# A vision tower on one core: value heads as stationaries of 32 or 64 columns, dealt over the strips of the array

## The chip, the cores and the metric

The kernel is written in Bass and runs on one core of a Trainium2 chip. A core has TensorE (PE, with its weight loads listed as PEld), VectorE (DVE), ScalarE (ACT), GpSimd (POOL), and SyncE (SP), which issues the transfers. The metric is the device time of one execution in microseconds (us).

## The reference

64 images of 84 by 84 pixels become 26 tokens each (a class token and 25 patches) of 192 features. Four layers follow, each an attention and a feed-forward block with a residual sum, all in fp32. Layer 2 has an attention inside its feed-forward block and so has layer 3, which makes six attentions. With `q`, `k`, `v` the projections of the normalised tokens, the part that matters here is the same in all six:

```
attn = einsum('bhqd,bhkd->bhqk', q, k)              # the scores, per image and head
attn = softmax / causal softmax / relative softmax / random features / integer softmax of it
out  = einsum('bhqk,bhkd->bhqd', attn, v)           # the value products
out  = out.transpose(0, 2, 1, 3).reshape(b, n, -1) @ proj_w + proj_b
```

| attention | heads x width | kind | time of it in the profile, us |
|---|---|---|---|
| L0 | 6 x 32 | causal, low rank | 76 to 163 |
| L1 | 12 x 64 | softmax with tables of relative positions for scores and values | 1662 to 1950 |
| L2a | 12 x 16 | random features (no exponent of the scores) | 2152 to 2304 |
| L2f | 12 x 16 | softmax | 2330 to 2427 |
| L3a | 12 x 16 | integer softmax, on VectorE alone | 2755 to 2857 |
| L3f | 12 x 16 | softmax, and a mix of tokens by a score, on GpSimd | 2884 to 3020 |

## The kernel before, in words

Everything is planned by hand: each engine has its own list of steps, and semaphores tie them. `attention()` writes all six attentions. It works on tiles of four images (4 x 26 = 104 tokens), 16 tiles in all. Four tiles make a turn (two in L1), so there are four turns (eight in L1). The lists `order` (PE, ACT) and `dve_order` (DVE) fix what comes after what within a turn, for instance on PE: values 0, v 2, scores 3, k, q, values 1, v 3, out of the last turn, scores 0 of the next, values 2, v 0, back, scores 1, values 3, v 1, back, scores 2. Engines are strictly in order, so a step that waits holds up all behind it.

The steps of one tile:

- **scores** (PE, L1673): for each image `im` (0 to 3) and each chunk `c` of heads (`NC` chunks: 2 in L0, L2f, L3a, L3f; 4 in L2a; 6 in L1), one product with a stationary of 32 columns (the image's 26 queries and padding). Its output goes to rows 32 `im` to 32 `im` + 31 of the bank, so `im` picks a strip of 32 columns of the array. The loop runs over images outside and chunks inside. In L1 `rel_scores` (L1683) does the same with a table of 40 columns.
- **shift, normalise** (DVE): subtract the maximum, sum, reciprocal, scale, transpose in blocks of 32. `exponents` (ACT) lies between them in the softmax kinds. In L1 both parts have some twenty small instructions more.
- **blocks** (ACT L1906, POOL L1622): the transposed weights of the four images are copied into a block-diagonal operand `p_bd` (in `n_tok`) of 104 rows and 104 columns per head.
- **v** (PE L595, then ACT L1888 and L1890, or L1895 in L1): the values of the tile are projected and written to `v_x`. Each head has 128 columns there, of which only its own 16 (32, 64) are not zero: the zeros are cleared once (POOL L1342, L1388) and the values are put at the place of the head among the output's rows. The last third of the heads is written twice, because the output projection wants those 64 rows in both halves.
- **values** (PE L1704): for each head one product of its 128 columns of `v_x` with `p_bd`, 104 columns, summed in PSUM over 8 heads, then over 4 heads. In L1 two heads and a product with the table `rel_table` (L1724) make one sum, six times. ACT L1943 or L1946 moves the result to `o_f`.
- **out, back**: the output projection, its transposes, and the sum with the residual on DVE (L2230).
- **spread** (DVE L2077): writes the keys of the next turn, one copy for each head with all other heads' rows zero. Scores of the next turn wait for it (`k_done`).

An fp32 product shows as two matrix passes in the trace, each with its own weight load: a tile of L2f has 12 products, 24 passes.

Of the kernel before, what the change touches and what calls it, by code (L numbers as in the profile page):

```python
# [25 lines left out]
IMG, SLOT = 64, 26  # L26
# [74 lines left out]
def vit_tower(nc, a, out, stop=99):  # L101
# [17 lines left out]
    with ctx:  # L119
# [68 lines left out]
        k_x = sb("k_x", [128, 12 * 416], scope=at)  # L188
        v_x = sb("v_x", [128, 2 * 1536 + 128], scope=at)
        z_t = [sb(f"z_t{j}", [128, 12, SLOT], scope=at) for j in range(2)]  # L190
# [1211 lines left out]
        def attention(cfg, res, *others, stats_too=True):  # L1402
# [132 lines left out]

            def spots(j, at, copies, copy_step, heads, step):
                part = v_x[:, 1536 * j + at:1536 * j + at + 1]
                return bass.AP(part.tensor, part.offset, [part.ap[0], [copy_step, copies], [step, heads], [1, d]])

# [107 lines left out]
            def tensor(pe):  # L1647
# [10 lines left out]
                def scores(i, g):  # L1658
                    t = G * i + g
                    pe.wait_ge(s_free.sem, s_free_at + t - 1)  # L1660
                    if g == 0 and cfg.kind == "causal" and i == 0:
                        keep_clock(bank[4], 8)
                    if g == 0:
                        pe.wait_ge(s["k_done"].sem, b["k_done"] + i + 1)
                        used(last_qk[0], i, last_qk[1])
                    o = bank[4 + g % 2]
                    for im in range(4):
                        m = SLOT * (4 * g + im)
                        for c in range(NC):
                            kx = key_rows(i, c * HCH, HCH).rearrange("p (h n) -> p h n", n=n)  # L1670
                            q0 = qcols(c, i).start + m
                            w = HCH * SLOT
                            ins = nc.tensor.matmul(o[32 * im:32 * im + 32, c * w:(c + 1) * w],  # L1673
                                                   q_t[0:R, q0:q0 + 32], kx[:, :, m:m + SLOT],
                                                   start=True, stop=True)
                    ins.then_inc(s["s_full"].sem, 1)

                def rel_scores(i, g):
                    o = job("rel", G * i + g, 0)
                    for im in range(4):  # L1680
                        m = SLOT * (4 * g + im)
                        for c in range(NC):
                            ins = nc.tensor.matmul(o[32 * im:32 * im + 32, 40 * c:40 * c + 40],  # L1683
# [13 lines left out]
                def values(t, g):  # L1697
# [3 lines left out]

                    def product(o, h, start, stop):
                        x0 = 1536 * (g % 2) + 128 * h
                        return nc.tensor.matmul(o, v_x[:, x0:x0 + 128], p_bd[g % 2][:, h, :], start=start, stop=stop)  # L1704
                    for v in range(halves):
# [4 lines left out]
                        if no == 2:  # L1710
                            for c, hs in enumerate((range(H * 2 // 3), range(H * 2 // 3, H))):
                                for h in hs:
                                    ins = product(ob[:, 104 * c:104 * c + 104], h, h == hs[0], h == hs[-1])
                        else:
# [3 lines left out]
                            for k in range(3):  # L1718
                                c, p = divmod(3 * v + k, 2)
                                o = ob[:, 104 * k:104 * k + 104]  # L1720
                                product(o, 2 * (3 * v + k), True, False)
                                product(o, 2 * (3 * v + k) + 1, False, False)
                                part = rel_mass[g][:, 128 * c:128 * c + 128].rearrange("p (b s) -> p b s", s=32)
                                ins = nc.tensor.matmul(o, rel_table[:, 128 * p:128 * p + 128], part[:, :, 0:SLOT],  # L1724
                                                       start=False, stop=True)
                        ins.then_inc(s["av_full"].sem, 1)
# [103 lines left out]
            def scalar(act):  # L1830
# [46 lines left out]
                def value_projection(t):  # L1877
# [3 lines left out]
                    for v in range(halves):  # L1881
                        p = job("v", t, v)[:, 0:WH]
                        if v == 0 and t > 1:
                            act.wait_ge(s["av_full"].sem, b["av_full"] + halves * (t - 1))
                        if no == 2:
                            low_heads = H * 2 // 3
                            ph = p.rearrange("p (u h d) -> p u h d", u=1, d=d)
                            nc.scalar.activation(spots(j, 0, 1, 0, low_heads, 128 + d), ph[:, :, 0:low_heads, :],  # L1888
                                                 ACT.Identity)
                            ins = nc.scalar.activation(spots(j, 128 * low_heads, 2, 64, H - low_heads, 128 + d),  # L1890
                                                       ph[:, :, low_heads:H, :].to_broadcast([128, 2, H - low_heads, d]),
                                                       ACT.Identity)
                        else:
                            ph = p.rearrange("p (k u d) -> p u k d", u=2, d=d)
                            ins = nc.scalar.activation(spots(j, 768 * v, 2, 192, 3, 256), ph, ACT.Identity)  # L1895
                        ins.then_inc(s["job_used"].sem, 1)

# [716 lines left out]
```

## Time and profile before

| | us |
|---|---|
| median of 3 runs | 3102.24 |
| lowest, highest | 3101.4, 3104.73 |
| span of the profiled execution | 3102.3 |
| PE busy | 2887.7 (93%) |
| PEld busy | 2668.6 (86%) |
| DVE busy | 2090.0 (67%) |
| ACT busy | 1075.2 (35%) |
| POOL busy | 616.9 (20%) |

The profile is of one execution. Busy times are unions of instruction spans. Matrix passes overlap, because each is listed with its latency, so how fast they follow one another is read from their starts: the length of a merged row, less the last pass, over the number of passes less one. Times in a window answer are from the span's start.

### The profile page before, as it was taken

How to read it: one execution, taken by the hardware profiler on the slowest of the kernel's cores; microseconds unless marked ns; L12 is line 12 of the kernel's file. 1: busy time of each engine (PE TensorE's matmuls, PEld its weight loads, DVE VectorE, ACT ScalarE, POOL GpSimd, SP SyncE). 2: the span in 40 equal slices, each digit the busy share in tenths (PEclk: the TensorE clock that was granted, in tenths of full speed). 3: DMA queues.
4: the chain of work that ended last, by engine and by line, in shares of the span. 5: the costliest groups of instructions: out<-in, count | busy, mean ns of one | idle time of the engine just before them, and what ended most of it. 6: DMA issues, size and time to landing. Idle time of an engine off the chain costs nothing. (4 is left out here: it accounts for less than half of the span.)

```text
span 3102.3 us, 56416 instructions
## 1 busy us (share of the span) xinstructions
PE 2887.7 (93%) x19925; PEld 2668.6 (86%) x19925; DVE 2090.0 (67%) x5299; ACT 1075.2 (35%) x2140; POOL 616.9 (20%) x807
## 2 busy tenths in 40 slices
PE   8889999999999999999997998896989889958888
PEld 7789999999999999999997888675778889957677
DVE  3867677777777777777776766333457667777876
ACT  2533333333333333233333333212445333334433
POOL 1312121212112121212112110112213101122450
PEclk9989999999999999999998999798999889989898
DMA  3001100000000000000000000371000100000000
GB/s 136 36 20 37 37 21 33 36 36 18 36 36 36 18 36 36 24 30 36 18 31 9 2 2 2 117 237 54 2 11 2 54 19 19 1 11 16 23 19 17
DMA packets 24461, 105.56 MB, mean 34 GB/s; under 512 B 4455, under 2 KB 9463, under 8 KB 19086
## 3 DMA queue, kind: packets, MB, share of 16 engines
q1 hardware_dynamic: 22654, 99.62, 9.2%
q0 software_dynamic: 1584, 3.30, 0.3%
q8 instruction: 99, 1.62, 0.2%
q14 instruction: 124, 1.02, 0.1%
HBM read 98.32 MB, written 6.64 MB: 34 GB/s over the span
## 5 line engine op out<-in xcount | busy, mean ns | idle before, releaser
L905 ACT ACTIVATE hid<-bank,dat 128x384 f32<-128x384 f32 (+1 forms) x912 | 554.4, 608 | 1147.9 <-PE bank L595 1033.3
L870 PE MATMUL bank<-w,hid_hi 128*128 128x384 f32 x2964 | 857.5, 361 | 2.2 <-DVE y_tok L921 1.6
L872 PE MATMUL bank<-w,hid_lo 128*128 128x192 f32 x2964 | 745.0, 251 | 0.0
L872 PEld LDWEIGHTS bank<-w,hid_lo 128*128 128x128 f32 x2964 | 570.2, 192 | 1.7
L870 PEld LDWEIGHTS bank<-w,hid_hi 128*128 128x128 f32 x2964 | 560.8, 189 | 5.7 <-issue 4.1
L939 DVE TENSOR_TENSOR hid_lo<-hid,hid_hi 128x384 fp32r<-128x384 f32 (+1 forms) x912 | 540.0, 592 | 31.5
L936 DVE CAST hid_hi<-hid 128x384 fp32r<-128x384 f32 (+1 forms) x912 | 340.9, 374 | 126.7 <-ACT hid L905 125.4
L962 DVE SCALAR_TENSOR_TENSOR h_tok<-bank,gate,h_tok 128x192 f32<-128x192 f32 x416 | 173.6, 417 | 246.8 <-PE bank L872 243.3
L595 PE MATMUL bank<-xa_hi,w_hi 128*128 128x384 f32 (+1 forms) x912 | 324.6, 356 | 7.3 <-DVE w_lo L748 4.4
L595 PE MATMUL bank<-xa_lo,w_hi 128*128 128x384 f32 (+1 forms) x912 | 323.2, 354 | 0.0
L595 PE MATMUL bank<-xb,w_lo 128*128 128x384 f32 (+1 forms) x912 | 322.7, 354 | 0.0
L595 PE MATMUL bank<-xa_hi,w_lo 128*128 128x384 f32 (+1 forms) x912 | 322.0, 353 | 0.0
L595 PE MATMUL bank<-xb,w_hi 128*128 128x384 f32 (+1 forms) x912 | 320.6, 352 | 0.0
L1704 PE MATMUL bank<-n_tok,v_x 128*128 128x104 f32 x2112 | 282.4, 286 | 27.7 <-ACT k_x L1911 14.7
L1704 PEld LDWEIGHTS bank<-n_tok,v_x 128*128 128x128 f32 x2112 | 265.2, 200 | 42.7 <-issue 17.1
L768 POOL TENSOR_TENSOR w_lo<-raw,w_hi 128x1536 fp32r<-128x1536 f32 x36 | 125.7, 3493 | 677.2 <-DVE hid_lo L939 677.2
L1622 POOL COPY n_tok<-p_x 32x312 f32<-32x312 f32 (+1 forms) x192 | 92.4, 481 | 579.0 <-DVE p_x L2192 448.2
L595 PEld LDWEIGHTS bank<-xa_hi,w_hi 128*128 128x128 f32 x912 | 172.8, 189 | 16.5 <-issue 5.0
L968 DVE SCALAR_TENSOR_TENSOR h_tok<-bank,gate,h_tok 128x192 f32<-128x192 f32 x416 | 173.7, 418 | 14.5
L595 PEld LDWEIGHTS bank<-xb,w_hi 128*128 128x128 f32 x912 | 172.8, 189 | 10.6
L595 PEld LDWEIGHTS bank<-xa_hi,w_lo 128*128 128x128 f32 x912 | 172.7, 189 | 9.9
L595 PEld LDWEIGHTS bank<-xb,w_lo 128*128 128x128 f32 x912 | 172.6, 189 | 9.8
(361 smaller groups left out, 4367.3 us busy)
## 6 DMA issues: line engine op xcount, KB each, us to landing
raw<-in_L_exp SPq DMA_DIRECT2D x36, 1344.0 KB, 5.7
w_e<-in_L_exp SPq DMA_DIRECT2D x20, 576.0 KB, 3.9
w_e<-in_L_exp SPq DMA_DIRECT2D x20, 384.0 KB
pix<-in_pixels SPq DMA_DIRECT2D x6, 832.0 KB, 10.3
w_e<-in_L_exp SPq DMA_DIRECT2D x20, 195.0 KB
raw<-in_L_mlp SPq DMA_DIRECT2D x2, 1344.0 KB, 6.5
wp_raw<-in_L_att SPq DMA_DIRECT2D x1, 2304.0 KB, 8.2
route_rows<-in_rows_clear SPq DMA_DIRECT2D x1, 2000.0 KB, 23.4
```

The lines of the kernel that those rows point to most:

```text
L595: ins = nc.tensor.matmul(o, l, r, start=start and n == 0, stop=stop and n == 4)
L768: nc.gpsimd.tensor_tensor(w1_lo[j][:, :, :], r1, w1_hi[j][:, :, :].bitcast(F32), ALU.subtract).then_inc(s["w_split"].sem, 1)
L870: nc.tensor.matmul(o[:, 0:2 * D], hid_hi[k % 2][:, m, c], w2[j][:, m, :], start=m == 0, stop=False)
L872: ins = nc.tensor.matmul(o[:, 0:D], hid_lo[k % 2][:, m, c], w2[j][:, m, 0:D], start=False, stop=m == HC - 1)
L905: nc.scalar.activation(hid[(6 * k + m) % 3][:, 0:128 * nt], bank[4 + (6 * k + m) % 4][:, 0:128 * nt], func, bias=bias).then_inc(s["h_act"] ...
L936: nc.vector.tensor_copy(hid_hi[k % 2][:, m, 0:w], h).then_inc(s["dve_step"].sem, 1)
L939: nc.vector.tensor_tensor(hid_lo[k % 2][:, m, 0:w], h, hid_hi[k % 2][:, m, 0:w].bitcast(F32), ALU.subtract).then_inc(s["h_split"].sem, 1)
L962: nc.vector.scalar_tensor_tensor(res[:, t, :], o[:, 0:D], g, res[:, t, :], ALU.mult, ALU.add).then_inc(s["dve_step"].sem, 1)
L968: nc.vector.scalar_tensor_tensor(res[:, t, :], o[:, D:2 * D], g, res[:, t, :], ALU.mult, ALU.add).then_inc(s["y_used"].sem, 1)
L1622: nc.gpsimd.tensor_copy(p_bd[t % 2][r, :, SLOT * im:SLOT * im + SLOT], p_x[t % 2][r, 0:H, 0:SLOT]).then_inc(s["bd_low"].sem, 1)
L1704: return nc.tensor.matmul(o, v_x[:, x0:x0 + 128], p_bd[g % 2][:, h, :], start=start, stop=stop)
```

## The change

Values of a head now stand in a cell of `max(32, d)` columns: 32 for heads of 16 and 32, 64 for heads of 64. With heads of 16 a cell holds a pair's 32 columns, one of the two heads in it and zeros for the other. The output rows are picked by the strip that the product goes to, not by zeros. In L0 and the 16-wide attentions, the last third of the heads is no longer stored twice but multiplied twice, once for each half. Products go over the strips in turn: with 12 heads of 16 there are 16 products instead of 12, 4 for each strip; with 6 heads of 32, 8 instead of 6, 2 for each strip; in L1 the 6 table products become 12 of 64 columns, so that a tile has 24 products over two strips instead of 18. ScalarE writes `v_x` with one instruction instead of two (as before in L1), and the clearing of `v_x` covers 1536 columns instead of 3200. In `scores` and `rel_scores` the loops change places: chunks outside, images inside.

```diff
-        v_x = sb("v_x", [128, 2 * 1536 + 128], scope=at)
+        v_x = sb("v_x", [128, 2 * 768], scope=at)
...
+            cell = max(32, d)
+            in_cell = cell // d
+            def value_cell(j, h):
+                x0 = 768 * j + cell * h
+                return v_x[:, x0:x0 + cell]
+            def value_spots(j, h0, heads):
+                part = value_cell(j, h0)[:, 0:1]
+                return bass.AP(part.tensor, part.offset, [part.ap[0], [cell * in_cell, heads // in_cell],
+                                                          [cell + d, in_cell], [1, d]])
...
-                    for im in range(4):
-                        m = SLOT * (4 * g + im)
-                        for c in range(NC):
-                            kx = key_rows(i, c * HCH, HCH).rearrange("p (h n) -> p h n", n=n)
+                    for c in range(NC):
+                        kx = key_rows(i, c * HCH, HCH).rearrange("p (h n) -> p h n", n=n)
+                        w = HCH * SLOT
+                        for im in range(4):
+                            m = SLOT * (4 * g + im)
                             q0 = qcols(c, i).start + m
...
-                    for im in range(4):
-                        m = SLOT * (4 * g + im)
-                        for c in range(NC):
+                    for c in range(NC):
+                        for im in range(4):
+                            m = SLOT * (4 * g + im)
                             ins = nc.tensor.matmul(o[32 * im:32 * im + 32, 40 * c:40 * c + 40],
...
-                    def product(o, h, start, stop):
-                        x0 = 1536 * (g % 2) + 128 * h
-                        return nc.tensor.matmul(o, v_x[:, x0:x0 + 128], p_bd[g % 2][:, h, :], start=start, stop=stop)
+                    def product(o, h, strip, start, stop):
+                        return nc.tensor.matmul(o[cell * strip:cell * strip + cell, :], value_cell(g % 2, h),
+                                                p_bd[g % 2][:, h, :], start=start, stop=stop)
...
-                            for c, hs in enumerate((range(H * 2 // 3), range(H * 2 // 3, H))):
-                                for h in hs:
-                                    ins = product(ob[:, 104 * c:104 * c + 104], h, h == hs[0], h == hs[-1])
+                            low_heads = H * 2 // 3
+                            for c in range(2):
+                                for y in range(in_cell):
+                                    for strip in range(4):
+                                        h = in_cell * strip + y if c == 0 else low_heads + in_cell * (strip % 2) + y
+                                        ins = product(ob[:, 104 * c:104 * c + 104], h, strip, y == 0, y == in_cell - 1)
...
-                                product(o, 2 * (3 * v + k), True, False)
-                                product(o, 2 * (3 * v + k) + 1, False, False)
+                                for u in range(2):
+                                    product(o, 2 * (3 * v + k) + u, u, True, False)
                                 part = rel_mass[g][:, 128 * c:128 * c + 128].rearrange("p (b s) -> p b s", s=32)
-                                ins = nc.tensor.matmul(o, rel_table[:, 128 * p:128 * p + 128], part[:, :, 0:SLOT],
-                                                       start=False, stop=True)
+                                for u in range(2):
+                                    r0 = 128 * p + 64 * u
+                                    ins = nc.tensor.matmul(o[64 * u:64 * u + 64, :], rel_table[:, r0:r0 + 64],
+                                                           part[:, :, 0:SLOT], start=False, stop=True)
...
-                            nc.scalar.activation(spots(j, 0, 1, 0, low_heads, 128 + d), ph[:, :, 0:low_heads, :],
-                                                 ACT.Identity)
-                            ins = nc.scalar.activation(spots(j, 128 * low_heads, 2, 64, H - low_heads, 128 + d),
-                                                       ph[:, :, low_heads:H, :].to_broadcast([128, 2, H - low_heads, d]),
-                                                       ACT.Identity)
...
+                        nc.scalar.activation(value_spots(j, HH * v, HH), p.rearrange("p (k u d) -> p k u d", u=in_cell, d=d),
+                                             ACT.Identity).then_inc(s["job_used"].sem, 1)
```

No step changes its place in the lists. What changes within them on PE is seen first in L2a, a turn in its steady state, before (output rows and columns of a product, and how many follow one another; L1673 is `scores`, L1704 `values`, L595 the projection v):

```order
L1673 MATMUL bank<-k_x,q_t 32x78 x16
L1704 MATMUL bank<-n_tok,v_x 128x104 x12
L595 MATMUL bank<-wp_hi,xs 128x192 x2
L595 MATMUL bank<-wp_lo,xs 128x192
L595 MATMUL bank<-wp_hi,xs 128x192
L595 MATMUL bank<-wp_lo,xs 128x192
```

The same place of PE in the changed kernel, where `scores` is L1683 and `values` L1714:

```order
L1683 MATMUL bank<-k_x,q_t 32x78 x16
L1714 MATMUL bank<-n_tok,v_x 32x104 x16
L595 MATMUL bank<-wp_hi,xs 128x192 x2
L595 MATMUL bank<-wp_lo,xs 128x192
L595 MATMUL bank<-wp_hi,xs 128x192
L595 MATMUL bank<-wp_lo,xs 128x192
```

Twelve products of full width became sixteen of 32 columns, right behind other products of 32 columns. The change of the loops in `scores` does not show in these rows: it alters which strip each of the sixteen goes to.

On PE in L1, before (L1683 is `rel_scores`, L1724 the table product):

```order
L1673 MATMUL bank<-k_x,q_t 32x52 x24
L1683 MATMUL bank<-dat,q_t 32x40 x24
L1704 MATMUL bank<-n_tok,v_x 128x104 x2
L1724 MATMUL bank<-k_x 128x104
L1704 MATMUL bank<-n_tok,v_x 128x104 x2
L1724 MATMUL bank<-k_x 128x104
```

And in the changed kernel (L1693 is `rel_scores`, L1740 the table product):

```order
L1683 MATMUL bank<-k_x,q_t 32x52 x24
L1693 MATMUL bank<-dat,q_t 32x40 x24
L1714 MATMUL bank<-n_tok,v_x 64x104 x2
L1740 MATMUL bank<-k_x 64x104 x2
L1714 MATMUL bank<-n_tok,v_x 64x104 x2
L1740 MATMUL bank<-k_x 64x104 x2
```

Three products of 128 columns became four of 64 columns, two for each half of the array.

## Rows read from the trace of the kernel before

**Rows 1.** Page, part 1: busy time, share of the span, instructions of each engine.

```profile
PE 2887.7 (93%) x19925; PEld 2668.6 (86%) x19925; DVE 2090.0 (67%) x5299; ACT 1075.2 (35%) x2140; POOL 616.9 (20%) x807
```

**Rows 2.** Windows, a steady turn each of L0, L1, L2a, L2f, L3a, L3f: stretch, length, busy times (instructions), PE clock, DMA.

```profile
95.10:115.70 20.60, 19.63 (x184) 17.16 (x183) 19.23 (x51) 11.51 (x36) 8.16 (x20) 1.00 0.01 2
...
1752.40:1787.50 35.10, 31.81 (x391) 29.90 (x392) 24.89 (x91) 12.85 (x32) 3.19 (x10) 1.00 0.01 2
...
2232.10:2269.40 37.30, 37.30 (x314) 29.59 (x313) 17.03 (x42) 15.79 (x38) 7.47 (x20) 1.00 0.01 1
...
2371.70:2394.60 22.90, 22.90 (x219) 20.41 (x218) 18.06 (x43) 12.74 (x34) 7.47 (x20) 1.00 0.00 1
...
2796.70:2820.40 23.70, 22.97 (x217) 20.32 (x217) 21.12 (x55) 11.05 (x30) 7.70 (x20) 1.00 0.01 2
...
2940.90:2972.30 31.40, 29.14 (x230) 25.51 (x230) 24.24 (x53) 12.94 (x34) 19.68 (x38) 0.90 0.00 1
```

**Rows 3.** Timeline of PE: scores of L0 (78 columns), then L2f (156 columns).

```profile
87.76 0.50 PE L1673 MATMUL bank<-k_x,q_t 96*32 96x78 f32 x16
...
2380.61 0.76 PE L1673 MATMUL bank<-k_x,q_t 96*32 96x156 f32 x16
```

**Rows 4.** Groups by line and form, PE: mean length of one pass of these scores.

```profile
L1673 PE MATMUL bank<-k_x,q_t 96*32 96x156 f32 x768 | 37.5, 308 | 12.6 <-issue 8.8 <-DVE k_x L2077 3.8
...
L1673 PE MATMUL bank<-k_x,q_t 96*32 96x78 f32 x768 | 34.0, 234 | 1.4 <-ACT q_t L1874 1.4
```

**Rows 5.** Timeline of PE in L2a: scores before values, scores alone, values alone.

```profile
2200.36 1.63 PE L1673 MATMUL bank<-k_x,q_t 96*32 96x78 f32 x32
2201.93 2.92 PE L1704 MATMUL bank<-n_tok,v_x 128*128 128x104 f32 x24
2204.63 0.45 PE L595 MATMUL bank<-wp_hi,xs 128*128 128x192 f32 x2
...
2205.13 0.27 PE L595 MATMUL bank<-wp_lo,xs 128*128 128x192 f32 x1
2205.34 1.63 PE L1673 MATMUL bank<-k_x,q_t 96*32 96x78 f32 x32
2206.90 0.44 PE L595 MATMUL bank<-xa_hi,wp_hi 128*96 128x416 f32 x1
...
2210.74 2.82 PE L1704 MATMUL bank<-n_tok,v_x 128*128 128x104 f32 x24
2213.34 0.45 PE L595 MATMUL bank<-wp_hi,xs 128*128 128x192 f32 x2
```

**Rows 6.** Timeline of PE in L1: scores and table scores of one tile, then values of another.

```profile
1666.72 1.79 PE L1673 MATMUL bank<-k_x,q_t 128*32 128x52 f32 x45
...
1668.48 1.39 PE L1683 MATMUL bank<-dat,q_t 128*32 128x40 f32 x44
1669.80 0.62 PE L595 MATMUL bank<-wp_hi,xs 128*128 128x384 f32 x2
...
1736.59 0.66 PE L1704 MATMUL bank<-n_tok,v_x 128*128 128x104 f32 x4 [1.62 <-ACT k_x L1911]
...
1740.60 0.60 PE L595 MATMUL bank<-wp_hi,xs 128*128 128x384 f32 x2
```

**Rows 7.** Timeline in L2f: scores, values, and what comes next.

```profile
2371.74 0.76 PE L1673 MATMUL bank<-k_x,q_t 96*32 96x156 f32 x16
...
2372.43 2.92 PE L1704 MATMUL bank<-n_tok,v_x 128*128 128x104 f32 x24
...
2375.13 0.45 PE L595 MATMUL bank<-wp_hi,xs 128*128 128x192 f32 x2
```

**Rows 8.** Timeline of PE in L3f: a turn's first tile, after a wait.

```profile
2940.88 1.29 PE L1673 MATMUL bank<-k_x,q_t 96*32 96x156 f32 x16 [2.30 <-issue]
2942.09 5.44 PE L1704 MATMUL bank<-n_tok,v_x 128*128 128x104 f32 x24
```

**Rows 9.** Instructions on `v_x`: its clearing on GpSimd (shortest, median, longest in ns).

```profile
L1342 POOL MEMSET v_x<- x3: 2764/2766/2768, 59.1 to 2726.8; 128x3200 f32 x3
```

More of the change, by code:

```diff
@@ L1534, in attention @@
                     .rearrange("p (h n) -> p h n", n=104) for j in range(2)]
-            def spots(j, at, copies, copy_step, heads, step):
-                part = v_x[:, 1536 * j + at:1536 * j + at + 1]
-                return bass.AP(part.tensor, part.offset, [part.ap[0], [copy_step, copies], [step, heads], [1, d]])
+            cell = max(32, d)
[7 more added lines that the diff above has]
+                                                          [cell + d, in_cell], [1, d]])
             def sync(sp):
@@ L1666, in scores @@
                     o = bank[4 + g % 2]
-                    for im in range(4):
-                        m = SLOT * (4 * g + im)
-                        for c in range(NC):
-                            kx = key_rows(i, c * HCH, HCH).rearrange("p (h n) -> p h n", n=n)
+                    for c in range(NC):
[3 more added lines that the diff above has]
+                            m = SLOT * (4 * g + im)
                             q0 = qcols(c, i).start + m
-                            w = HCH * SLOT
                             ins = nc.tensor.matmul(o[32 * im:32 * im + 32, c * w:(c + 1) * w],
@@ L1884, in value_projection @@
                             act.wait_ge(s["av_full"].sem, b["av_full"] + halves * (t - 1))
-                        if no == 2:
-                            low_heads = H * 2 // 3
-                            ph = p.rearrange("p (u h d) -> p u h d", u=1, d=d)
-                            nc.scalar.activation(spots(j, 0, 1, 0, low_heads, 128 + d), ph[:, :, 0:low_heads, :],
-                                                 ACT.Identity)
-                            ins = nc.scalar.activation(spots(j, 128 * low_heads, 2, 64, H - low_heads, 128 + d),
-                                                       ph[:, :, low_heads:H, :].to_broadcast([128, 2, H - low_heads, d]),
-                                                       ACT.Identity)
[L1893 to L1896, printed above, removed]
+                        nc.scalar.activation(value_spots(j, HH * v, HH), p.rearrange("p (k u d) -> p k u d", u=in_cell, d=d),
+                                             ACT.Identity).then_inc(s["job_used"].sem, 1)
                 def blocks(t, g):
```

## The prediction

> **What bounds the kernel now.** I read the page's first part, then windows of one steady turn of each attention, then the timeline of PE inside these turns. The page shows PE busy 93% and every other engine far below [rows 1], but that is a mean over stages, and this change touches only the six attentions, some 700 of 3102 us. There the windows decide [rows 2]. In L2a PE is busy 37.30 of 37.30 us while DVE has 17.03: PE alone is the bound. In L1 PE has 31.81 of 35.10 and DVE 24.89. In L2f it is 22.90 of 22.90 against 18.06. In L3a DVE has 21.12 of 23.70 and in L0 19.23 of 20.60, so there VectorE is nearly or fully the bound already. L3f has 24.24 of 31.40 on DVE.
>
> DVE also loses a little at each instruction. L0's turn has 51 instructions and 1.37 us without work, so I take 0.027 us each as a floor. The shortest possible turn by DVE is then 27.3 us in L1 (24.89 + 91 x 0.027), 18.2 in L2a, 19.2 in L2f, 22.6 in L3a, 25.7 in L3f and 20.6 in L0.
>
> **What a strip costs.** The scores already use strips. In L0 16 passes of 78 columns start within 0.50 - 0.23 = 0.27 us, in L2f 16 of 156 columns within 0.76 - 0.30 = 0.46 us [rows 3, 4] (0.30 for the last pass at full clock; the mean of 308 ns has some slower ones in it). One after another even 78 columns could not follow at 0.018 us: the four strips work side by side. With 4 passes to a strip there are 4 rounds, 3 steps between them, so 78 more columns cost (0.46 - 0.27) / 3 = 0.065 us a round: 0.83 ns a column and pass. A round of 52 columns is then 0.046 us, of 78 0.067, of 104 0.089, of 156 0.13, with 2 ns for each pass on top. In L2a the same 78 columns need (1.63 - 0.23) / 31 = 0.045 us a pass instead of 0.018 [rows 4, 5]. What differs is that 8 passes in a row go to one strip, not 4. I read from this that about four passes can stand ready for a strip and the next one holds up the rest. The new order puts only 2 in a row on a strip, so L2a and L1 gain there, while L0, L2f, L3a and L3f (4 in a row, already side by side) gain nothing from the exchanged loops.
>
> A pass of full width takes 0.11 us: 24 passes of values in L2a start within 2.82 - 0.27 = 2.55 us [rows 5]. By its 104 columns it would be 0.089, so the load of 128 weight columns sets it. With 32 columns the load is no longer in the way.
>
> **The change part by part, in PE time.**
>
> *Values, heads of 16.* Before: 2.60 us from the first pass to the next step (2210.74 to 2213.34) [rows 5]. After: 16 products are 32 passes, 8 rounds. Four rounds at 104 columns are 0.27 + 0.19 x 26 / 78 = 0.33, four more 4 x 0.089 = 0.36, together 0.69. Then the step back to full width: the last score pass of L2a starts at 2205.34 + 1.40 = 2206.74 and the next step at 2206.90, 0.16 us [rows 5]. The step into strips costs 0.10 (2205.13 to 2205.34 is 0.21, an ordinary step 0.11). Sum 0.95, saved 1.65. Where scores stand right before values, no second step in is needed: in L2f the pair is now 2371.74 to 2375.13, 3.39 us [rows 7], then 0.46 + 0.13 + 0.69 + 0.18 = 1.46, saved 1.93.
>
> The Trainium skill (TensorEngine Tiling (Array Packing), Key Properties) says that changing the tiling mode drains TensorE. That speaks against this change, which adds two such steps to values that have no scores before them. Hangs on that sentence: the trace agrees, and the 0.10 and 0.16 above are its price here.
>
> *Scores of L2a.* 2205.34 to 2206.90 is 1.56 us; 8 rounds of 0.067 and 0.16 are 0.70: saved 0.86. A pair of scores and values is 2200.36 to 2204.63, 4.27 us [rows 5], then 0.54 + 0.07 + 0.69 + 0.18 = 1.48, saved 2.79. A turn has three pairs, one scores and one values alone: 3 x 2.79 + 0.86 + 1.65 = 10.9 us.
>
> *Scores of L1.* 1666.72 to 1669.80, 3.08 us for 48 and 48 passes [rows 6]. Strips alone would ask 12 x 0.046 + 12 x 0.036 = 0.98. But 96 passes in 0.98 us is 0.010 each, faster than any row; the best is 0.018. From the other side, the fastest long row here is 1.39 us for 44 passes, 0.027 each, 2.6 us for all. I take 0.014 x 96 + 0.13 = 1.5, near the short rows, since that long row has two strips at most at work; saved 1.55 (bounds 0.4 and 1.9).
>
> *Values of L1.* 1736.59 to 1740.60, 4.01 us for 36 passes [rows 6]. After: 48 passes, 24 to each of two strips, 24 x 0.089 = 2.14, and 0.2 for the steps: saved 1.65. No row shows a strip of 64 columns. If the loads of both halves stood in line, it would be the load time of now, 24 x 0.11 = 2.7, saved 1.1. A turn saves 2 x (1.55 + 1.65) = 6.4.
>
> *Values of L0.* 12 passes (1.25 us by 0.11 a pass) become 16, 4 rounds: 0.33 + 0.26 = 0.6, saved 0.65.
>
> *Beside other work.* ScalarE writes `v_x` once instead of twice; ACT is busy 15.79 of 37.30 in L2a at most [rows 2], worth nothing. The clearing of `v_x` shrinks from 2.77 us to 2.77 x 1536 / 3200 = 1.33, four times [rows 9], in front of the staging on POOL and before the first tile; PE projects keys then, so I count nothing (at most 4 x 1.4).
>
> **How much reaches the end.** Where PE stays the bound, all of it; elsewhere until DVE's floor.
> - L2a: a turn 37.3 - 10.9 = 26.4, far above 18.2. ScalarE has squares, blocks and four exponents in line behind the shorter PE steps, 0.5 us lost. Two steady turns 2 x 10.4, and of the 21.6 that remain in the first and last turn some 60%: 34.
> - L1: 35.1 - 6.4 = 28.7, above 27.3, 0.4 lost. Six steady turns 6 x 6.0, and 4 at the ends: 40. The 1.62 us in which PE waits for the evicted mass stay.
> - L2f: 22.9 falls to 19.2 and some 0.7 where DVE waits for an exponent that ScalarE can only begin when the shift is done: saved 3.0 and 2.5 in the steady turns. 1.5 at the start, 6 in the last turn, where two blocks of values stand one behind the other with DVE idle (2 x 1.65) and half the pipeline is a steady turn: 13.
> - L3a: 23.7 to 22.6 and 0.2: 0.9 twice, 5 at the ends: 7.
> - L3f: 31.4 to 25.7 and 0.7. Here values also cost 5.44 us at half clock [rows 8], the granted clock of the turn being 0.90. 5.0 twice, 8 at the ends: 18.
> - L0: DVE stays the bound: 3 at its ends.
>
> Sum 34 + 40 + 13 + 7 + 18 + 3 = 115. The profiled execution spans 3102.3 us, the median of the runs is 3102.24, so both come to 2987.
>
> **Rivals.**
>
> *Products can't be supplied so fast.* Behind the short rows stands 0.027 us a pass, 0.055 a product. Then L1's scores save 0.4 instead of 1.55 (16 x 1.15 = 18), L2a's scores and values take 0.88 each instead of 0.54 and 0.69 (16 x 0.53 = 8), and DVE hides most of the rest (3): 29 less, 3016. For it: no row with more than 16 passes is faster. Against: those rows are explained by their strips. The Trainium skill (TensorE: Matmul & The Clock Gate, Wait — 56ns, not 53.3ns?) gives about 62 ns for each MATMUL when the sequencer decodes it in software. By it L1's 48 products take 3.0 us, as now, and the time would be about 3025. Against that page's case: 8 products in 0.27 us in L0 are 34 ns each [rows 3].
>
> *All of PE's saving arrives.* Blocks saved: L2a 43, L1 51, L2f, L3a and L3f 16 x 1.65 + 12 x 0.28 = 30 each, L0 10: 194, time 2908. Against it: DVE's floors.
>
> *The clock falls.* In L3f the waits of 2.3 us are followed by a stretch at half clock [rows 8]. With PE idle more in L0, L2f and L3a such stretches come there too, each doubling some 3.4 us of PE work. Those turns have 4 to 8 us of slack then, so the cost falls on L1 and L2a, 12 turns x 3.4 = 41: 3028. For it, L1 waits 1.62 us in each turn; against, its clock is 1.00 nearly throughout [rows 2].
>
> *Slower: products of 128 rows don't run side by side in the strips.* The rows that do have 96 rows (L0, L2f). In L1, with 128 rows, the scores show only partial overlap. If each pass takes its 0.089 us alone, values of 16-wide heads are 32 x 0.089 + 0.26 = 3.1 against 2.60, L1's 48 x 0.089 + 0.2 = 4.5 against 4.01, and L0's 1.7 against 1.35. That is 0.5 x 16 in L2a, L1, L2f and L3f each and half of it in L3a and L0, 40 us, less 14 for L2a's scores: 3128. It decides from about 0.070 us a pass, where values save nothing: 32 x 0.070 + 0.26 + 0.1 = 2.6.
>
> **How the numbers follow.** Forecast 68%, its own range 2955 to 3012. Supply 15% (3016), all arrives 4% (2908), clock 10% (3028), slower 3% (3128). The range 2948 to 3034 leaves out the last, the second and tails of the others. A measurement of this kernel tells 0.2%, 6 us, from no change. Faster 0.95, within 0.02, slower 0.03.
>
> **What would show it.** A block of values in L2a of 32 passes within some 0.9 us, and its scores within 0.8. L1's scores of about 1.5 us between first pass and next step (2.6 would be the supply rival). A turn of L2a near 27 us, of L1 near 29, of L2f near 20, with PE no longer filled in L2f, L3a and L0 and DVE's idle time near 0.03 us an instruction. Wrong would be: values blocks above 1.5 us, a turn of L0 or L3a that is longer than now, or a granted clock below 0.9 in L1 or L2a.

## The result and the profile after

The changed kernel takes 2985.52 us (median of 4 runs, 2982.65 to 2989.68) against 3103.36 us (3101.4 to 3104.73, 4 runs) for the kernel before on the same chip: a ratio of 0.9623, 95% interval 0.961 to 0.9637. It is faster by 3.8%; the forecast was 2987. The profiled execution spans 2987.9 us, 114.4 less than before.

The page's first part, which answers to [rows 1]:

```profile
PE 2719.2 (91%) x20693; PEld 2465.2 (83%) x20693; DVE 2088.5 (70%) x5299; ACT 1061.3 (36%) x2060; POOL 620.7 (21%) x807
```

PE has 768 matmuls more and 168.5 us less to do. More of them lie beside each other now. DVE has the same 5299 instructions and the same work. So 54 us of PE's gain did not reach the end, and the windows show in which attentions.

Windows of a steady turn of L0, L1 (a quick and a slow one), L2a, L2f, L3a and L3f, to be laid beside [rows 2] (stretch, length, busy times of PE, PEld, DVE, ACT, POOL with instructions, PE clock, DMA share, GB/s):

```profile
95.00:117.60 22.60, 20.34 (x199) 15.46 (x198) 19.15 (x50) 10.74 (x30) 7.45 (x20) 0.83 0.01 2
...
1743.50:1771.40 27.90, 24.61 (x417) 22.36 (x418) 25.26 (x92) 12.85 (x32) 5.10 (x10) 1.00 0.01 2
...
1799.00:1830.60 31.60, 26.56 (x418) 24.12 (x420) 25.30 (x92) 12.85 (x32) 5.11 (x10) 0.95 0.01 2
...
2170.30:2197.20 26.90, 26.80 (x347) 17.82 (x346) 16.88 (x42) 15.23 (x34) 7.51 (x20) 1.00 0.01 2
...
2286.20:2305.00 18.80, 16.01 (x252) 12.45 (x253) 17.58 (x43) 11.86 (x31) 7.46 (x20) 1.00 0.01 2
...
2697.00:2719.10 22.10, 17.16 (x252) 13.61 (x253) 20.98 (x55) 10.37 (x27) 7.70 (x20) 0.92 0.01 2
...
2831.70:2859.90 28.20, 22.29 (x262) 17.14 (x263) 24.29 (x53) 11.99 (x30) 20.20 (x38) 0.88 0.01 1
```

Only L2a is still filled by PE, 26.80 of 26.90 us. In L2f, where PE was busy throughout, it now has 16.01 of 18.80 while DVE has 17.58. In L1's quick turn DVE has 25.26 of 27.90. Its idle 2.64 us over 92 instructions are 0.029 each, near the 0.027 that the prediction took for DVE's floor. In L1's longer turn both engines have idle time and the clock is 0.95. L3f stands at 28.20 with DVE at 24.29, so something else holds it. L0's turn has become longer, 22.60 us instead of 20.60, with DVE's work as before and the granted clock at 0.83; the turn behind it went from 23.0 to 20.7 us, so the two together are 43.3 instead of 43.6.

PE's timeline in L2a: scores, values right behind them, the next step, and scores alone (start, length, line, operation, stationary, moving and output form, count). It answers to [rows 5]:

```profile
2172.82 0.75 PE L1683 MATMUL bank<-k_x,q_t 96*32 96x78 f32 x32
2173.38 0.90 PE L1714 MATMUL bank<-n_tok,v_x 128*32 128x104 f32 x32
2174.21 0.47 PE L595 MATMUL bank<-wp_hi,xs 128*128 128x192 f32 x2
...
2175.16 0.75 PE L1683 MATMUL bank<-k_x,q_t 96*32 96x78 f32 x32
2175.84 0.43 PE L595 MATMUL bank<-xa_hi,wp_hi 128*96 128x416 f32 x1
```

The pair starts at 2172.82 and the next step at 2174.21: 1.39 us, where 1.48 was predicted and it was 4.27 before. The scores alone take 0.68 against 1.56, predicted 0.70.

PE's timeline in L1, scores with table scores, then the first rows of a block of values and the step behind it. It answers to [rows 6]:

```profile
1777.45 0.76 PE L1683 MATMUL bank<-k_x,q_t 128*32 128x52 f32 x48
1778.03 0.65 PE L1693 MATMUL bank<-dat,q_t 128*32 128x40 f32 x48
1778.61 0.36 PE L1799 MATMUL bank<-o_hi,wp_hi 128*128 128x208 f32 x1
...
1784.84 0.40 PE L1714 MATMUL bank<-n_tok,v_x 128*64 128x104 f32 x4 [1.63 <-ACT k_x L1917]
1785.04 0.38 PE L1740 MATMUL bank<-k_x 128*64 128x104 f32 x4
...
1787.13 0.45 PE L595 MATMUL bank<-wp_hi,xs 128*128 128x384 f32 x1
```

The scores take 1.16 us (3.08 before, 1.5 predicted), the values 2.29 (4.01 before, 2.34 predicted). The 1.63 us in front of the values, in which PE waits for the evicted mass, stayed as said.

For each attention I took the time from its first score pass to the first transpose of the phase behind it, and, from the same trace, how long the granted clock stood at the lower of its two levels, 1.2 instead of 2.4 GHz (in brackets), in us:

```
                      L0          L1           L2a          L2f         L3a         L3f          sum
before             90.9 (9)   292.1 (24)   143.1 (3)    97.7 (3)   105.8 (9)   139.5 (25)   869.1 (73)
changed            90.7 (26)  245.2 (25)   109.2 (13)   84.0 (17)   97.1 (34)  133.7 (47)   759.9 (162)
saved               0.2        46.9         33.9        13.7         8.7         5.8        109.2
predicted           3          40           34          13           7          18          115
```

The other 5.2 us of 114.4 lie outside the attentions. No run shows where they come from. The clock is at half for 162 us in the attentions instead of 73.

### The profile page after: what moved, and what is told of

The parts are those of the page before. It is cut to its first block and busy times, and to the rows that moved or that the text cites. A ratio compares the mean times of both kernels' runs of the same rounds, so it can differ in the third digit from the quotient of the medians.

```text
span 2987.9 us, 57872 instructions
## 1 busy us (share of the span) xinstructions
PE 2719.2 (91%) x20693; PEld 2465.2 (83%) x20693; DVE 2088.5 (70%) x5299; ACT 1061.3 (36%) x2060; POOL 620.7 (21%) x807
## 3 DMA queue, kind: packets, MB, share of 16 engines
q8 instruction: 105, 1.72, 0.2%
## 5 line engine op out<-in xcount | busy, mean ns | idle before, releaser
L939 DVE TENSOR_TENSOR hid_lo<-hid,hid_hi 128x384 fp32r<-128x384 f32 (+1 forms) x912 | 539.8, 592 | 31.5
L595 PE MATMUL bank<-xa_hi,w_hi 128*128 128x384 f32 (+1 forms) x912 | 324.5, 356 | 8.3 <-DVE w_lo L748 5.1
L595 PE MATMUL bank<-xa_lo,w_hi 128*128 128x384 f32 (+1 forms) x912 | 323.0, 354 | 0.0
L595 PE MATMUL bank<-xb,w_lo 128*128 128x384 f32 (+1 forms) x912 | 322.4, 353 | 0.0
L595 PE MATMUL bank<-xa_hi,w_lo 128*128 128x384 f32 (+1 forms) x912 | 321.7, 353 | 0.0
L595 PE MATMUL bank<-xb,w_hi 128*128 128x384 f32 (+1 forms) x912 | 320.2, 351 | 0.0
L595 PEld LDWEIGHTS bank<-xa_hi,w_hi 128*128 128x128 f32 x912 | 172.6, 189 | 18.3 <-issue 5.7
L595 PEld LDWEIGHTS bank<-xb,w_hi 128*128 128x128 f32 x912 | 172.6, 189 | 10.6
L763 POOL CAST w_hi<-raw 128x1536 fp32r<-128x1536 f32 x36 | 52.8, 1466 | 618.1 <-DVE hid_lo L939 564.6
L595 PEld LDWEIGHTS bank<-xa_hi,w_lo 128*128 128x128 f32 x912 | 172.5, 189 | 9.9
L595 PEld LDWEIGHTS bank<-xb,w_lo 128*128 128x128 f32 x912 | 172.3, 189 | 9.8
L595 PEld LDWEIGHTS bank<-xa_lo,w_hi 128*128 128x128 f32 x912 | 172.9, 190 | 8.5
```

The lines of the kernel that those rows point to most:

```text
L595: ins = nc.tensor.matmul(o, l, r, start=start and n == 0, stop=stop and n == 4)
L763: nc.gpsimd.tensor_copy(w1_hi[j][:, :, :], r1).then_inc(s["w_split"].sem, 1)
L939: nc.vector.tensor_tensor(hid_lo[k % 2][:, m, 0:w], h, hid_hi[k % 2][:, m, 0:w].bitcast(F32), ALU.subtract).then_inc(s["h_split"].sem, 1)
```

## Experiments

All ratios are to the kernel before, on the same chip; "the changed kernel" is the one above.

**The two parts by themselves.** The first run is the kernel before with the exchanged loops alone (the same exchange in `rel_scores`):

```diff
-                    for im in range(4):
-                        m = SLOT * (4 * g + im)
-                        for c in range(NC):
-                            kx = key_rows(i, c * HCH, HCH).rearrange("p (h n) -> p h n", n=n)
+                    for c in range(NC):
+                        kx = key_rows(i, c * HCH, HCH).rearrange("p (h n) -> p h n", n=n)
+                        w = HCH * SLOT
+                        for im in range(4):
+                            m = SLOT * (4 * g + im)
...
-                            w = HCH * SLOT
```

> The kernel before with the exchanged loops of scores and rel_scores alone (values keep their 128 columns). Theory (four strips side by side, about four passes can stand ready for each): L2a's block of scores falls from 1.40 to 0.52 us between first and last start, L1's scores and table scores from 3.08 to 1.2 us as in the changed kernel, L0, L2f, L3a and L3f keep theirs. PE bounds L2a and L1, so 16 x 0.88 and 16 x 1.9 us arrive nearly whole: about 43 us off 3103, ratio 0.986. Rival (the gain of the change is all in values, the loops only shift which pass waits): ratio 1.00.

Measured 3058.4 us, 0.9858 (0.9834 to 0.9881): by the ratio 44 us saved. The same 32 passes that took 1.63 us in [rows 5], on PE's timeline of this run:

```profile
2200.69 0.75 PE L1673 MATMUL bank<-k_x,q_t 96*32 96x78 f32 x32
```

The second is the changed kernel with the old loops of the scores, so that the values alone differ from before (the diff above, read backwards).

> The changed kernel with the old order of loops in scores and rel_scores (values dealt over strips). Theory: what is left of 117 us without the loops' part, some 75 us, ratio 0.976; the two parts add up because both lie on PE in L2a and L1, and only in L1 a little less than the sum, as DVE becomes the bound there. Rival (the parts hide each other behind DVE): this kernel alone gives over 95 us.

Measured 3018.02 us, 0.9724 (0.9708 to 0.974): 86 us saved, where 75 were expected. The parts make 44 + 86 = 130 and together 117. The missing part lies mostly in L1. There the exchange alone saves 32.7 (292.1 to 259.4) and the values alone 33.0 (to 259.1), but both 46.9 (to 245.2; 240.0 in the second profile of the changed kernel, further down). That is 19 (14) us less than the sum. Taken singly, each part arrives whole in L1's steady turns: 35.1 - 2 x 1.92 = 31.3 us for the scores and 35.1 - 2 x 1.72 = 31.7 for the values, and the turns are 31.3 and 31.6. Both together would make 27.8, and the quick turns (27.6 and 27.9) have that; what is lost is lost in the slower ones, up to 31.5 us.

**How deep a strip can be filled.** The next two take the changed kernel and give each strip eight, then four passes in a row, instead of two. Nothing else changes: the same products, forms and counts.

```diff
-                            for c in range(2):
-                                for y in range(in_cell):
-                                    for strip in range(4):
+                            for strip in range(4):
+                                for c in range(2):
+                                    for y in range(in_cell):
```

> The changed kernel with the strip as the outermost loop in values of the four 16-wide attentions: 8 passes in a row go to one strip instead of 2; the same products, loads and columns. Theory of four places for each strip: the next strip begins when the fifth pass of the last one starts, so a block lasts (3 x 4 + 8) x 0.089 = 1.8 us between first and last start instead of 0.67. L2a pays 16 x 1.1 = 18 us whole, L2f, L3a and L3f some 20 together: 3022, ratio 0.974. Rival (TensorE looks over the whole queue and takes what is free): no change, 0.962. Rival (narrow loads alone give the gain, strips side by side nothing): no change either.

```diff
-                                for y in range(in_cell):
-                                    for strip in range(4):
+                                for strip in range(4):
+                                    for y in range(in_cell):
```

> The changed kernel with the head of a pair as the innermost loop in values of the 16-wide attentions: 4 passes in a row to one strip instead of 2. Theory of four places for each strip: nothing changes, a block of values stays at 0.67 us, ratio 0.962 as the changed kernel. Rival (every pass behind another on its strip holds up the rest): a block of 1.0 us or more and a ratio near 0.968.

Eight in a row: 3011.9 us, 0.9702 (0.9686 to 0.9718). Four in a row: 2990.59, 0.9639 (0.9622 to 0.9655), which the interval does not tell from the changed kernel. PE's timeline in L2a, a block of values behind scores with eight in a row and the step behind it:

```profile
2207.70 2.04 PE L1714 MATMUL bank<-n_tok,v_x 128*32 128x104 f32 x32
2209.67 0.47 PE L595 MATMUL bank<-wp_hi,xs 128*128 128x192 f32 x2
```

Such a block with four in a row:

```profile
2171.09 0.95 PE L1714 MATMUL bank<-n_tok,v_x 128*32 128x104 f32 x32
2171.97 0.47 PE L595 MATMUL bank<-wp_hi,xs 128*128 128x192 f32 x2
```

From the first to the last start 32 passes behind scores take 0.646 us with two in a row, 0.698 with four and 1.785 with eight (1.8 was expected); blocks that stand alone take 0.668, 0.707 and 1.808. The step lies between four and eight, as the prediction had read from L0's and L2a's scores. This is the direct test of that reading, since only the order differs. The single starts show the places too: with eight in a row there is, at each change of strip, a pass 0.006 us behind the fifth of the last strip (0.387 behind 0.381 us, 0.774 behind 0.768, 1.161 behind 1.155, counted from the first start of a block that stands alone), where rounds on one strip are 0.089 apart. I read these passes as the first of the next strip; the trace does not name the strip.

It is also a probe of the floors. Eight in a row puts 16 x 1.14 = 18 us of PE work back into each of L2a, L2f, L3a and L3f. L2a grew by 13.2, L2f by 6.1, L3a by 3.2, and L3f was 2.2 shorter. The expectation, 18 for L2a and some 20 for the other three, was too high: 3022 us against 3011.9. In all four, time at half clock fell as well (L3f 24 us against 47), so these sizes are not PE work alone. In L2a's steady turns, at full clock in both kernels, 4.2 to 4.3 of the 4.6 us arrive (26.3 to 30.5 and 26.9 to 31.2).

**L1: is the wait for the mass what is left?** In the changed kernel the step that adds the mass comes ahead of the output step in PE's list of L1:

```diff
-                         ("v", 0, 1), ("scores", 1, 1), ("exp", 0, 1), ("out", 0, -1), ("bd", 1, 0), ("mass", 1, 0),
+                         ("v", 0, 1), ("scores", 1, 1), ("exp", 0, 1), ("bd", 1, 0), ("mass", 1, 0), ("out", 0, -1),
```

> The changed kernel with one step of L1's list moved: blocks 1 and mass 1 stand before the output projection of the last turn, on PE and on ScalarE. Theory (PE still bounds L1's turns of 31 us or shares the bound with DVE): the wait of 1.6 us for the evicted mass before values 1 lies under the 4 us of the output projection; turns that PE bounds get up to 1.9 us shorter, those that DVE bounds (27.6 us, its busy time and gaps being 27.4) nothing: 6 to 10 us in all, ratio 0.960. Rival (DVE bounds every turn of L1 now): 0 to 2 us, 0.962.

Measured 2990.01 us, 0.9632 (0.9619 to 0.9645), L1 244.1 us instead of 245.2: no gain. PE's waits for the evicted mass in L1 fell from 10.0 us in six to 1.9 in one, so the theory that they cost L1 time has fallen; they stood in slack. L1's time itself is less steady than this difference: eight profiles of kernels with the same L1 program, among them the two of the changed kernel, have 240.0 to 246.5 us, with no fixed relation to their 15 to 27 us at half clock. That DVE bounds the turns fits its busy time; no run takes DVE work out of L1, so it is not shown.

**L3f: what took the place of PE.** The missed term of the sum. Waits of DVE in the whole of L3f, the kernel before (engine, tile, line, what it waited for; us in total, times, longest):

```profile
DVE y_tok L2230 <- PE bank L1797: 20.0, 6, 5.2
DVE m L2151 <- PE bank L1673: 7.4, 6, 3.1
```

The changed kernel:

```profile
DVE y_tok L2236 <- PE bank L1813: 9.3, 3, 6.7
DVE o_f L2210 <- POOL feat L1604: 6.7, 3, 3.8
...
DVE o_f L2210 <- ACT k_t L1873: 2.4, 1, 2.4
DVE m L2157 <- PE bank L1683: 2.2, 3, 1.6
```

The two waits for PE shrank from 27.4 to 11.5 us, and 9.1 us of a new one appeared. DVE's splitting of the output (L2210) now waits for GpSimd's mixing of the images (L1604). The third row says ACT, but its place in the timeline shows the same GpSimd work. POOL and then DVE, one turn of the changed kernel:

```profile
2841.05 2.38 POOL L1604 TENSOR_TENSOR feat<-feat,o_f 128x208 f32<-128x208 f32 x4
...
2843.56 1.25 DVE L2210 TENSOR_TENSOR o_f<-o_f,spare_low 128x832 f32<-128x832 f32 x1 [2.38 <-ACT k_t L1873]
```

GpSimd is done at 2843.43 and DVE starts at 2843.56. The experiment lets DVE do the shift of one tile and the normalising of another ahead of the split, and gives GpSimd's step for the next images a place of its own:

```diff
+                if cfg.mix:
+                    dve_order = [("normalise", 1, 0), ("shift", 3, 0), ("normalise", 2, 0), ("split", 0, -1),
+                                 ("pool", 0, 0)] + dve_order[4:]
...
-                        if cfg.mix and g == 2:
-                            pool_images(i)
+                    elif name == "pool":
+                        pool_images(i)
```

> The changed kernel with DVE's list of L3f changed alone: shift 3 and normalise 2 stand before the split of the last turn's result, which waits for GpSimd's mixing, and the pooling of the mix behind it. Theory (the missing 10 us of L3f went into DVE's wait of 2.4 us a turn for GpSimd's last multiplication): L3f gets 5 to 8 us shorter, 133.7 to 127, ratio 0.960. Rival (the granted clock, half of full for 47 of L3f's 134 us, holds it back): under 2 us, 0.962.

Measured 2979.89 us, 0.9617 (0.96 to 0.9635). Waits of DVE in its L3f:

```profile
DVE y_tok L2239 <- PE bank L1816: 9.6, 3, 4.4
DVE m L2160 <- PE bank L1686: 2.6, 4, 1.8
...
DVE o_f L2213 <- POOL feat L1607: 1.1, 1, 1.1
```

The wait for GpSimd fell from 9.1 to 1.1 us and L3f from 133.7 to 127.9. So this wait held 5.8 of the 12 us that the prediction has too much there.

A run from above says more on L3f. The kernel with the exchanged loops alone has the wide values of before, and in this profile the two steady turns were at full clock:

```profile
2870.60:2898.50 27.90, 25.42 (x228) 22.06 (x230) 23.46 (x50) 13.06 (x34) 20.04 (x38) 1.00 0.01 2
2898.50:2926.80 28.30, 26.02 (x233) 22.67 (x235) 24.09 (x53) 13.07 (x34) 19.70 (x38) 1.00 0.01 1
```

In the kernel before the same turns took 30.9 and 31.5 us at clocks of 0.89 and 0.90, in the changed kernel 28.3 and 28.3. So wide values at full clock already gave what L3f's steady turns gained, 62.4 to 56.2 us against 56.6, and L3f as a whole took 134.8 us against 139.5 before and 133.7 changed. DVE did not wait for GpSimd at the split there. How much of the 5.8 us the narrow values gave, and how much a different place of the half-clock stretches, no run tells apart.

**Both orders, and both kernels again.** The two changes of order together:

```diff
+                if cfg.mix:
+                    dve_order = [("normalise", 1, 0), ("shift", 3, 0), ("normalise", 2, 0), ("split", 0, -1),
+                                 ("pool", 0, 0)] + dve_order[4:]
...
+                         ("v", 0, 1), ("scores", 1, 1), ("exp", 0, 1), ("bd", 1, 0), ("mass", 1, 0), ("out", 0, -1),
```

> The changed kernel with both moves of the last two expectations on the lists (mass before the output projection in L1; shift and normalise before the split in L3f). They lie in different attentions, so the gains add: ratio 0.958 if each gives its theory's middle, 0.962 if neither does.

2984.33 us, 0.9618 (0.9605 to 0.9631); L3f 127.5, L1 244.2: as a whole the 0.962 that was expected if neither change helps. The next two are the changed kernel and the one with the later split, unchanged, side by side on one chip (no edit).

> The changed kernel once more, beside the next run: ratio 0.962 as before, so that the two can be compared.

> The kernel with L3f's split later once more. In its profile L3f was 5.8 us shorter; the run as a whole must show 4 to 6 us against the changed kernel on the same chip, 0.960 against 0.962, unless the shorter L3f was a matter of that one execution's clock.

2985.34 us (2980.94 to 2989.16), 0.9621 (0.9605 to 0.9638), and 2984.95 (2981.17 to 2991.42), 0.9622 (0.9605 to 0.9639). L3f is 133.9 and 128.0 us: three profiles of three with the later split show it some 6 us shorter. Yet the whole kernels cannot be told apart; the 4 to 6 us that were expected do not show. In the two profiles of this pair L3a went the other way, 97.4 to 100.0, with 43 instead of 34 us at half clock. I have no version that beats the changed kernel by more than its measurement tells.

**The clock.** In L0, L2f, L3a and L3f the changed kernel gets an idle-time filler: one more product of 428 columns, whose result nobody reads, before PE waits for a tile's weights.

```diff
+                    if cfg.kind not in ("rel", "performer") and t >= G:
+                        pe.wait_ge(s["av_used"].sem, b["av_used"] + t - NA + 1)
+                        keep_clock(bank[av_banks[t % NA]], 1)
```

> The changed kernel with one extra full-width product of 428 columns (two passes, 0.7 us) written to the free bank before PE waits for a tile's blocks, in values of L0, L2f, L3a and L3f from the second turn on. It only keeps PE at work. Theory (the clock's fall costs a few us, as PE has slack where it falls): half-clock time in these four attentions falls from 124 to under 60 us, and their sum from 405 us by 3 to 8. Rival (the clock doesn't matter, and the product delays values): half-clock time falls, the sum rises by 5 or more.

2990.59 us, 0.9644 (0.9631 to 0.9658): no gain. Time at half clock in the four attentions fell from 124 to 97 us, not to under 60 as expected, and their sum rose from 405.5 to 412.4. The theory has missed and the rival's rise of 5 or more came. The filler's own work cost more than 27 us less at half clock gave back; what half clock costs by itself this run does not say.

**Is it DVE that bounds L0, L2f and L3a?** The changed kernel without DVE's multiplication of the weights by their reciprocal sum in these three, so their weights are not normalised (the counts of DVE's steps follow):

```diff
-                        link(nc.vector.tensor_tensor(p, p, bc(sm.unsqueeze(2), n3), ALU.mult))
+                        if cfg.kind not in ("causal", "log2") and cfg.dram != "L2_fat":
+                            link(nc.vector.tensor_tensor(p, p, bc(sm.unsqueeze(2), n3), ALU.mult))
```

> The changed kernel without DVE's multiplication by the reciprocal of the sum in L0, L2f and L3a (the weights stay unnormalised there): one instruction a tile less, 0.32 us in L0 and 0.48 in the others, with 0.03 between instructions 16 x (0.35 + 0.51 + 0.51) = 22 us of DVE's time. Theory (after the change DVE bounds these three, whatever the clock does): 16 to 22 us come off their sum of 271.8, ratio 0.956. Rival (the granted clock, half of full in 76 of these 272 us, or the way over ScalarE and GpSimd bounds them): under 10 us, 0.960.

2970.16 us, 0.9573 (0.9556 to 0.959). A steady turn of its L2f, in the columns of the windows above:

```profile
2278.20:2295.00 16.80, 15.60 (x249) 12.42 (x248) 15.62 (x39) 11.80 (x30) 7.47 (x20) 1.00 0.01 2
```

Four DVE instructions of 1.96 us together went, and the turn is 2.00 us shorter. L0 gave 5.2, L2f 7.9, L3a 7.0: 20.1 of the 22 us expected. DVE's work counts nearly in full in these three attentions, while in L2f and L3a PE's 18 us (the run with eight in a row) counted 6.1 and 3.2.

## Why the prediction was right, and where it was not

The forecast of 2987 holds, and the first of its two readings is shown: strips work side by side, for products of 128 rows and for the values too. The second is shown in part. The bound goes over to DVE in L0, L2f and L3a, as the run with less DVE work shows; L2a stays with PE. In L1 DVE's floor and PE's sum give nearly the same turn, and L3f's saving did not come as it was worked out. Point by point:

- *Values of 16-wide heads.* From the first pass to the next step in L2f and L2a 0.69 plus the drain was predicted; the passes themselves take 0.668. The Trainium skill (TensorEngine Tiling (Array Packing), Key Properties) says that changing the tiling mode drains TensorE. The trace agrees: on the way back to full width the next step starts 2174.21 - 2173.38 - 0.646 = 0.18 us after the last start, the 0.18 that the prediction used. Between scores and values, both of 32 columns, there is none: the values begin 0.05 us after the last score pass.
- *Scores of L1*, the mis-sized term: 1.5 us was taken, 1.16 measured. The 96 passes start 0.012 apart on the average, where I took 0.014 and 0.13 for the steps. The bound of 0.98 from strips alone was nearer than the short rows. The 0.34 us are 0.34 x 16 = 5.4 us of PE over L1, which came out 6.9 better than the 40 in the first profile and 12 in the second; that the one made the other is not shown.
- *L1's turn.* 28.7 and 0.4 was predicted, above DVE's floor of 27.3; the quick turns of the changed kernel's two profiles have 27.1 to 28.7 us. With the scores at 1.16, PE's sum is 27.8, so these turns do not tell the two bounds apart. The turns of 30.9 to 31.5 in the first profile have stretches at half clock (0.94 and 0.95), but the second has one of 30.2 at full clock, so the clock is not the whole reason.
- *L2a*: 34 predicted, 33.9 measured; *L2f* 13 and 13.7; *L3a* 7 and 8.7. L2f's turns of 17.9 and 18.7 went below the floor of 19.2, and L3a's of 22.1 below 22.6. In L2f DVE's idle time per instruction was as assumed (1.22 us in 43), but its own work was 17.58 instead of 18.06.
- *L3f* is the step that failed: "31.4 to 25.7 and 0.7 ... 5.0 twice, 8 at the ends: 18". Measured are 30.9 and 31.5 to 28.3 and 28.3 in the steady turns, 5.8, and nothing at the ends: the first turn is 25.6 and the rest behind the last turn's start 51.5 us, both unchanged. I took DVE's floor as the next bound and did not ask what DVE itself waits for once PE is early. GpSimd is busy 19.68 of 31.40 us there [rows 2], and DVE's split stands behind its mixing. The later split shows 5.8 us of the 12. The starting point was misread as well: the 31.4 stands at a granted clock of 0.90, and the same wide values at full clock make turns of 27.9 and 28.3 (the run with the exchanged loops alone). The prediction saw the half clock there but counted the whole stretch as something that narrow values would end. The other 6 us stay open. L3f also has 47 us at half clock instead of 25. No run takes that away without adding work, but the run with eight in a row, with 24 us at half clock and 18 us more PE work, had L3f 2.2 us shorter, which suggests that the clock has a part in it.
- *L0*: 3 predicted at the ends, 0.2 measured. PE's 0.89 us per block (first to last start 1.205 to 0.312) brought nothing, while L0's time at half clock rose from 9 to 26 us.
- *The sum* was right within 2 us because L3f's 12 and L0's 3 too much stood against 7 in L1, 2 in L2f and L3a, and 5 outside the attentions, for which I counted nothing. That the errors cancel to 2 us is luck. The terms were not all good.
- *The signs of being wrong*: no block of values at full clock is above 1.5 us in the 16-wide attentions, and L1 and L2a as a whole keep a clock of 0.95 and 0.94. Two signs did come, in single turns. L0's turn is 22.6 us instead of 20.6 (the next is shorter by 2.3), and L1's first two turns have clocks of 0.85 and 0.88 (before 0.87 and 1.00). Neither tells against the strips. The clock fell in both turns; that it made them longer is not shown.

The rivals: *Supply of products* has fallen. 48 products start within 1.16 us, 24 ns each, against the 55 ns that it rests on. The Trainium skill (TensorE: Matmul & The Clock Gate, Wait — 56ns, not 53.3ns?) has about 62 ns for a software-decoded MATMUL. No block of short products here shows it. *128 rows don't run side by side* has fallen with 0.668 us for 32 passes. *All arrives* has fallen: in L0, L2f and L3a by DVE's floor. *The clock falls* is half true. The stretches came, 162 us instead of 73, but where it said the price falls on L1 and L2a with 41 us, L2a met its 34 and L1 beat its 40.

## What to carry to other kernels

Products with narrow stationaries run side by side in the array's strips, if the program deals them out: change the strip with each product. Four passes in a row on one strip were nearly as good here, eight held up the rest. Count what a shorter engine saves only down to the next engine's floor, its busy time and what it loses per instruction. Then look once more for what *that* engine waits for, a third engine among it, since its waits were hidden while it was late anyway. And look at the granted clock of the turn from which a saving is counted: L3f's turn of 31.4 us at 0.90 was 28.3 at full clock with the same products.

## What the runs showed of the hardware that was not expected

- Over four strips passes can start some 0.01 us apart for long: in L1 48 score passes take 0.549 us from first to last start (0.0117 each) and 48 table passes 0.451 (0.0096), where no row before had less than 0.018.
- The order of the same 32 passes alone sets their time: 0.646, 0.698 and 1.785 us behind scores for two, four and eight in a row on a strip. About four passes seem to stand ready for a strip: at eight in a row the next strip, as read from the starts, begins right behind the fifth pass of the last.
- Stationaries of 64 columns load side by side as well. L1's values take 2.29 us for 48 passes, what their columns ask (24 rounds of 0.089 us and the steps), and no more for the loads.
- The faster PE had its clock lowered more often: 162 us at half clock in the attentions instead of 73, and the mean granted clock of the span fell from 0.955 to 0.940. No run isolates what that cost. A sign of it, from one profile of each kernel: L3f's steady turns with wide values take 30.9 and 31.5 us at 0.89 and 0.90, and 27.9 and 28.3 at 1.00.
